# Splitting the attention weights of groups 1 to 3 during attention, in place, in a two-FFN and attention kernel

## The reference

```
x = x + 0.5 * ffn(layernorm(x))        # phase f1
x = x + attention(layernorm(x))        # phase at
x = x + 0.5 * ffn(layernorm(x))        # phase f2

ffn(x): logits = x @ router_w + router_b            # 8 experts, top 2, softmax of the two
        h_e    = silu(x @ expert_w[e] + expert_b[e])
        out    = sum_e(weight_e * h_e) @ proj_w + proj_b
        y = x + out;  return norm_w * y / rms(y)

attention(x): q, k, v = x @ wq.T, x @ wk.T, x @ wv.T    # 16 query heads, 4 kv heads, head dim 128
        q, k = rope(q), rope(k);  k = k * key_weights[head]
        scores = q @ k.T / sqrt(128), causal;  out = (softmax(scores) @ v) @ wo.T
```

## Time and profile before

| | |
|---|---|
| median of 3 runs | 890.74 us |
| the profiled execution | 892.65 us |
| its span, first to last instruction | 890.8 us |
| mean granted TensorE clock | 0.971 |
| busy: PE / DVE / POOL / ACT | 822.6 / 701.0 / 585.2 / 521.4 us |
| phases: f1, attention, f2 | 0 to 171, 171 to 744, 744 to 891 us |
| HBM read and written | 22.02 and 12.58 MB |

### The profile page before, as it was taken

The page is one execution under the profiler, slowest core; times in us unless marked ns, Lnnn a source line. Parts: engine busy times, 40 slices in busy tenths (PEclk is TensorE's granted clock), DMA queues, the critical chain, the costliest instruction groups (busy, mean ns, idle before and its releaser), DMA issues. The chain is left out here.

```text
span 890.8 us, 17017 instructions
## 1 busy us (share of the span) xinstructions
PE 822.6 (92%) x4848; PEld 724.0 (81%) x4848; DVE 701.0 (79%) x1824; ACT 521.4 (59%) x1252; POOL 585.2 (66%) x444
## 2 busy tenths in 40 slices
PE   5998888767999999999999999999999998999984
PEld 4776776656889999999999899899999986787873
DVE  6899989899776776776866867767767797789987
ACT  3654534445765765755865766756767663554542
POOL 3667746368587687777777787777777812556743
PEclk9999988978999999999999999999999999899998
DMA  8053153410212311312312312212212100000001
GB/s 302 1 178 105 72 201 142 142 36 12 49 24 59 106 24 35 94 35 59 94 24 47 94 24 71 85 33 47 71 41 54 25 1 29 1 1 24 24 1 47
DMA packets 26673, 55.98 MB, mean 63 GB/s; under 512 B 3568, under 2 KB 9840, under 8 KB 25104
## 3 DMA queue, kind: packets, MB, share of 16 engines
q1 hardware_dynamic: 26640, 55.59, 21.4%
HBM read 22.02 MB, written 12.58 MB: 39 GB/s over the span
## 5 line engine op out<-in xcount | busy, mean ns | idle before, releaser
L1050 POOL TENSOR_TENSOR at_ql<-at_rot,at_qh 128x512 fp32r<-128x512 f32 x62 | 79.8, 1287 | 99.6 <-ACT at_qh L1272 99.6
L1289 ACT ACTIVATE at_pr<-at_sm,at_low 128x512 f32<-128x512 f32 (+3 forms) x256 | 140.4, 555 | 0.9 <-DVE at_low L1137 0.8
L1295 ACT ACTIVATE at_pth<-at_pt 128x512 fp32r<-128x512 f32 (+1 forms) x192 | 95.8, 525 | 76.0 <-PE at_pt L1449 75.2
L603 ACT ACTIVATE f_s<-f_ex,f_cols 128x512 f32<-128x512 f32 x128 | 84.1, 686 | 86.0 <-PE f_ex L751 46.3
L293 POOL TENSOR_TENSOR f_acc<-f_acc,f_u 128x512 f32<-128x512 f32 x68 | 100.8, 1509 | 40.8 <-DVE f_u L482 27.7
L1147 DVE TENSOR_SCALAR at_pr<-at_pr,at_inv 128x128 f32<-128x128 f32 (+3 forms) x256 | 113.1, 504 | 2.3
L1137 DVE CUSTOM_DVE_ANT_0 at_sm<-at_sc,at_mask 128x512 f32<-128x512 f32 (+3 forms) x256 | 109.8, 484 | 2.5 <-issue 2.4
L1152 DVE TENSOR_TENSOR at_ptl<-at_pt,at_pth 128x512 fp32r<-128x512 f32 (+1 forms) x192 | 108.7, 593 | 1.7 <-ACT at_pth L1295 1.5
L1059 POOL TENSOR_TENSOR at_rot<-ga,cos 128x512 f32<-128x512 f32 x78 | 104.2, 1336 | 4.1 <-POOL at_ql L1050 2.4
L1065 POOL TENSOR_TENSOR at_rot<-at_rot,gc 128x512 f32<-128x512 f32 x78 | 101.5, 1301 | 8.1 <-POOLq L1082 2.1
L1449 PE MATMUL at_pt<-ident,at_pr 128*128 128x128 f32 x640 | 96.3, 278 | 9.3 <-DVE at_pr L1147 6.8
(11 more groups left out here) (212 smaller groups left out, 2262.7 us busy)
## 6 DMA issues: line engine op xcount, KB each, us to landing
gc<-ga SPq DMA_DIRECT2D x160, 128.0 KB, 2.3
ga<-in_attn_w SPq DMA_DIRECT2D x4, 1280.0 KB, 7.7
attn_split<-gb SPq DMA_DIRECT2D x4, 1280.0 KB, 9.6
attn_split<-gc SPq DMA_DIRECT2D x4, 1280.0 KB, 12.1
gb<-attn_split SPq DMA_DIRECT2D x8, 512.0 KB, 4.2
at_wo<-attn_split SPq DMA_DIRECT2D x8, 512.0 KB, 4.3
x<-in_x SPq DMA_DIRECT2D x4, 512.0 KB, 9.0
e_raw<-in_expert_w SPq DMA_DIRECT2D x8, 256.0 KB, 6.7
```

What stands on the lines that cost most here:

```text
L1289: act.activation(pr[h % 2][:, cols], sm[h % 2][:, cols], ACT.Exp, bias=low[h % 2][:, i:i + 1], scale=-1.0, accum_out=tot[h % 2][:, i:i + 1 ...
```

## The change

Group 0 is still split in block 0 of f1, but only its 1536 key, query and value columns, in parts of 512 and 1024, straight into `wa` and `gb`; nothing goes to DRAM. All else is split in attention, in chunks of 512 columns (`CHUNK`) that go through one buffer, `stage`. A group has five: WO_A, WO_B (the two halves of its own wo), and WA, WB_A, WB_B of the next group's key, query and value weights. For each chunk SP loads `stage` after a swap (`load_chunk`, having waited that the chunk before is done), POOL scales the query columns (three of five), ACT copies to hi, DVE subtracts to lo and raises `w_lo`. The host stores the weights in chunks for that. Since chunks sit at fixed steps of a group, the attention loop now runs over groups: 4 steps of group 0, a loop over groups 1 and 2 with 4 steps in it, 4 steps of group 3.

The core of the diff:

```
+        CHUNK_AT = {(0, 1): WO_A, (0, 3): WO_B, (2, 0): WA, (2, 2): WB_A, (3, 0): WB_B}     # (j, h)
...
             def swaps(g, j):                                                                # SP
...
-                    if r == 1 and new_proj is not None:
-                        load_proj(new_proj, wa, FIRST, wa_in)
-                    if r == 3 and new_wo is not None:
-                        load_wo(new_wo)
-                    if r == NR - 1 and new_proj is not None:
-                        load_proj(new_proj, wb, LATER, wb_in)
+                    if j == 0 and r == 0:
+                        load_chunk(g - 1, WB_B)
+                    if j == 0 and r == 3:
+                        load_chunk(g, WO_A)
+                    if j == 1 and r == 4:
+                        load_chunk(g, WO_B)
+                    if j == 2 and r == 2 and more:
+                        load_chunk(g, WA)
+                    if j == 3 and r == 3 and more:
+                        load_chunk(g, WB_A)
...
                 rotate(s, 0)                                                                # POOL, rope(g, j)
+                if j == 0:
+                    scale_chunk(g - 1, WB_B)
                 for r in range(1, NR):
                     rest(s, r - 1)
                     rotate(s, r)
+                    if r == 2 and j == 2 and more:
+                        scale_chunk(g, WA)
+                    if r == 3 and j == 3 and more:
+                        scale_chunk(g, WB_A)
...
+            def chunk_rest(g, k):                                                           # DVE
+                hi, lo = chunk_parts(k)
+                dve.wait_ge(w_hi, chunk_number(g, k) + 1)
+                dve.tensor_tensor(lo, stage[:], hi.bitcast(F32), ALU.subtract).then_inc(w_lo, 1)
...
                     if h == G - 1 and not last:
                         value_rest(s + 1)
+                    if (j, h) in CHUNK_AT and (more or j == 0):
+                        chunk_rest(g, CHUNK_AT[j, h])
...
                     out_lead(n, s, h)                                                       # ACT
                     if more1:
                         prob_lead(n + 1, h1, 2)
+                    if (j, h) in CHUNK_AT and (more or j == 0):
+                        chunk_lead(g, CHUNK_AT[j, h])
                     if h > 0 and ahead:
                         rotated_lead(s + 1, h + 1)
                     if h == G - 1 and ahead:
                         value_lead(s + 1)
...
+            def chunk_split(g, k):                                                          # PE
+                pe.wait_ge(w_lo, chunk_number(g, k) + 1)
...
                 for h in range(G):
+                    if more and j == 2 and h == G - 1:
+                        chunk_split(g, WA)
+                    if more and j == 3 and h == 0:
+                        chunk_split(g, WB_A)
+                    if more and j == 3 and h == 1:
+                        chunk_split(g, WB_B)
+                    if j == 1 and h == 0:
+                        chunk_split(g, WO_B)
                     if more2:
                         scores(n + 2, s if h + 2 < G else s + 1, h2)
...
 # key, query h == 1, output: the waits on wa_in, wb_in and wo_in go
-                pe.wait_ge(wa_in, 32 * (t // BATCH) + WA0)
-                    pe.wait_ge(wb_in, 32 * (t // BATCH) + 32)
-                pe.wait_ge(wo_in, 32 * (s // BATCH) + 32)
...
-                if first:                                                                   # f1: POOL, ACT, DVE
-                    scale_queries(i)
+                if first and not prev:
+                    scale_queries()
-                    if first and e in group_at:
-                        group_lead(i, group_at.index(e))
+                    if first and not prev and e in group_at:
+                        group_lead(group_at.index(e))
-                    if first and e in group_at:
-                        group_rest(i, group_at.index(e))
+                    if first and not prev and e in group_at:
+                        group_rest(group_at.index(e))
```

More of the change, by code:

```diff
@@ L36 @@
 GW = C * QKV + G * D
+CHUNK = SEQ
+CHUNKS = GW // CHUNK
 COLS = C * E + C * D + E * C
@@ L620, in squares, with group_lead @@
                     act.activation(sq[:, t, :], y[:, t, :], ACT.Square, accum_out=ss[:, t:t + 1]).then_inc(sq_done, 1)
[L622 to L628, removed]
+            def group_lead(part):
+                act.wait_ge(a_scaled, (1, 3)[part])
+                act.activation(a_hi[part], a_raw[part], ACT.Copy).then_inc(a_hi_done, 1)
             def step_out(k):
@@ L1001, in _, with load_chunk, swaps @@
         def _(sp):
[L1002 to L1012, removed]
-            def swaps(s, new_wo=None, new_proj=None):
+            def load_chunk(g, k):
+                n = chunk_number(g, k)
+                if not (isinstance(n, int) and n == 0):
+                    sp.wait_ge(w_lo, n)
+                row = (g, CHUNKS - 2 + k) if k in (WO_A, WO_B) else (g + 1, k - WA)
+                sp.dma_start(stage[:], d["attn_w"][bass.ds(row[0], 1), row[1]].rearrange("o p n -> (o p) n")).then_inc(w_raw, 16)
+            def swaps(g, j):
+                s = BATCH * g + j
+                more = not isinstance(g, int) or g < KV - 1
                 for r in range(NR):
@@ L1089, in _ @@
             rstd(1)
-            with pool.Fori(1, STEPS) as s:
-                rest(s - 1, NR - 1)
-                rope(s)
+            for j in range(1, BATCH):
+                rope(0, j)
+            with pool.Fori(1, KV - 1) as g:
+                for j in range(BATCH):
+                    rope(g, j)
+            for j in range(BATCH):
+                rope(KV - 1, j)
             rest(STEPS - 1, NR - 1)
@@ L1299, in out_lead, with chunk_lead, step @@
                 act.activation(out_parts(s, h)[0], o_ps[:], ACT.Copy).then_inc(oh_done, 1)
-            def step(s, first, ahead):
+            def chunk_lead(g, k):
+                n = chunk_number(g, k)
+                act.wait_ge(w_raw, 16 * (n + 1))
+                if k in (WO_A, WO_B):
+                    if not (isinstance(g, int) and g == 0):
+                        act.wait_ge(xu_done, 2 * BATCH * g)
+                else:
+                    act.wait_ge(w_scaled, 3 * g + k - WA + 1)
+                act.activation(chunk_parts(k)[0], stage[:], ACT.Copy).then_inc(w_hi, 1)
+            def step(g, j, first, ahead):
+                s = BATCH * g + j
+                more = not isinstance(g, int) or g < KV - 1
                 for h in range(G):
@@ L1496, in output, with step @@
                     r.then_inc(pj_ready, 1)
-            def step(s, first, ahead):
+            def chunk_split(g, k):
+                pe.wait_ge(w_lo, chunk_number(g, k) + 1)
+            def step(g, j, first, ahead):
+                s = BATCH * g + j
+                more = not isinstance(g, int) or g < KV - 1
                 for h in range(G):
```

203 lines of the change are left out of this document (105 added, 98 removed).

## The result

The changed kernel takes 926.87 us (median, 925.77 to 930.70), beside 890.68 us (890.57 to 891.22) for the kernel before on the same chip: a ratio of 1.0413, 95% interval 1.0382 to 1.0444. It is 36.2 us slower; 28.5 was forecast, and 926.87 lies in the range and at the upper end of the forecast's own. The profiled execution took 927.54 us around a span of 925.7, 34.9 more than the span before.

The account below looks back on a forecast made before the run. The prediction took DVE to fill the first phase and PE alone to bound attention. -10.6 + 2.0 + 14.4 + 8.7 + 14.0 = +28.5 us on 890.7 gave 919.2 us, own range 911 to 927, 8 in 10 903 to 933.

Parts of the forecast that it names:

- WO_B: Step j=1, head 0: PE waits ahead of its scores for DVE's subtraction, 3.6 us in each of four groups, 14.4 us.
- WB_B: Step j=3, head 1: PE waits ahead of its scores for DVE's subtraction, 2.9 us in each of three groups, 8.7 us.
- the other work: Attention: seventeen chunks' copies, subtractions and products fit into ACT, DVE and POOL; with the longer code 2.0 us, 0 to 9.
- the clock: After seven new PE waits in attention the clock falls to 1.2 GHz, 2.0 us each: 14.0 us, 0 to 24.
- The shorter first phase: First feed-forward phase: DVE sheds weight splits, a gain of 10.6 us, between 9.6 and 12.8.
- the last block: Last batch block of the first feed-forward phase: loses between 2.96 and 4.96 us, taken as 3.8.
- Rival 1: Attention: the seven waits come but the clock stays high; 905.2 us, chance 0.15.
- rival 2: Attention: the clock stays low for the long stretch after each wait, 9.8 us more; 929.0 us, chance 0.08.
- The longer code: Attention as more step bodies in a row, with a four-step loop: 0.4 us; by the skill's rule 0 to 2 more.
- Rival 4: Attention's longer code is no longer held, some fifteen more instruction packets hold PE, 14 us more; 933 us, chance 0.05.
- Rival 3: Attention: splits are done before PE reaches the waits, so only the first phase's gain shows; 882.1 us, chance 0.06.
- signs of error: Attention: PE's waits under 1.5 us, the clock staying at 1.00, or other steps growing by more than 0.5 us each.

Follow-up runs that it names:

- e7_narrow: Kernel before, ACT copy and DVE subtraction of groups 1 to 3 in the first phase cut to 16 of 1280 columns, transfers kept: 882.24 us, ratio 0.9894.
- e4_fill: Changed kernel, PE making the coming head's scores once for nothing ahead of the WO_B and WB_B waits: 917.77 us, ratio 1.0300.
- e2_wo: Changed kernel with only the WO_B wait moved to right before the output projection: 913.21 us, ratio 1.0247.
- e5_flat: e1_use with the loop over groups 1 and 2 written out on all engines: 893.58 us, ratio 1.0029.
- e8_afterflat: Changed kernel, early waits kept, with the loop over groups 1 and 2 written out: 925.84 us, ratio 1.0386.
- e9_placedloop: e6_placed with the loop over groups kept, so one jump back per engine: 885.39 us, ratio 0.9925.
- e6_placed: e5_flat with ACT's copies behind rotated query and value, most DVE subtractions ahead of a normalisation, WB_B started a step earlier: 882.24 us, ratio 0.9890.
- e10_actback: e6_placed with ACT's chunk copies put back ahead of the rotated query and the value: 887.45 us, ratio 0.9944.
- e3_wb: Changed kernel with only the WB_B wait moved to right before the query projection of head 1: 915.98 us, ratio 1.0282.
- e1_use: Changed kernel with all four kinds of chunk wait moved to right before the matmuls that read the weights: 896.99 us, ratio 1.0078.

## Why the prediction was right, step by step

The direction, the mechanism and the place were right: seven waits of PE for DVE's subtraction, and a low clock behind them. The sum of 28.5 stands against 34.9 in the spans. That the time still lies inside the forecast's own range, by 0.1 us, is in part luck: the jump and the other work were put some 9 us too low and WB_B 3 too low, while the clock was put 2.5 too high and step 0 happened to be short. Term by term:

- **The shorter first phase**, forecast -10.6, measured -10.66; blocks 1 and 2 took 32.10 and 33.51 us. That the work of splitting fills it, and not the transfers, is shown by e7_narrow. For the last block I wrote 3.8, "the middle" of 2.96 and 4.96; the middle is 3.96.
- **WO_B**, forecast 14.4: 13.8 us of idle, 3.4 to 3.5 each. A step with this wait and no low clock (the last group's) is 37.83, 3.5 over 34.30. Right.
- **WB_B**, forecast 8.7: a step with it and no low clock is 38.2 (e4_fill), 3.9 over; 11.6 for three. Nearly all of the 1.0 us each is the subtraction itself: 1.66 us in the row below, where I had priced it at 0.69 by L1162. DVE and POOL at that place:

```profile
310.92 0.41 DVE L1164 TENSOR_TENSOR at_ptl<-at_pt,at_pth 128x256 fp32r<-128x256 f32 x1
311.25 1.66 DVE L1189 TENSOR_TENSOR gb<-stage,gb 128x512 fp32r<-128x512 f32 x1
```

```profile
311.10 1.26 POOL L1051 TENSOR_TENSOR at_rot<-ga,cos 128x512 f32<-128x512 f32 x1
312.32 1.73 POOL L1053 TENSOR_TENSOR gc<-gc,sin 128x512 f32<-128x512 f32 x1
```

  It begins inside POOL's product, seems to get going when that ends at 312.36, and lasts 0.55 more; POOL's next takes 1.73, where the one after it takes 1.28. The subtraction of L1162 takes one operand from PSUM, this one both from SBUF. The 17 chunk subtractions took 20.7 us, not 11.7. The Trainium skill (SBUF — State Buffer, SBUF: two separate sides) says that a DVE operation with two SBUF inputs and a GpSimd one that reads SBUF share a port pair under an exclusive lock, and whichever starts second fully blocks. These rows agree with it roughly (0.55 us are left of a subtraction of 0.69); no run took POOL's product away. It did not enter my sum, and it should have.
- **The clock**, forecast 14.0 for seven stalls: 11.5 by e4_fill. Six of seven fell, for 1.5 to 2.6 us each. Rival 1 is refuted, and rival 2 as well, since it asked for 3.4 each. The price is not fixed: against the step lengths of e4_fill it was 2.5 to 3.0 us each in e2_wo, where the low clock lasted longer.
- **The longer code**, forecast 0.4: this is the step that was mis-sized. Step 8 is 6.3 us over, of which the excess of an ordinary j = 0 step is 0.6; the other 5.7 are the jump, 2.6 idle and most of the rest a half clock behind it (2.7 by e4_fill). Rival 4 put the price on code that is merely new; that fell, since written-out code (e5_flat, e8_afterflat) has no such stall and on q8 not even more packets, 37. The prediction has the loop before jump thirteen times; over steps 1 to 13 it jumps back twelve times, and no wait of PE is put down to it. The Trainium skill (Runtime: NRT & Kernel Launch, Instruction fetch mechanics) says that prefetch is sequential and that a taken branch to code outside the current window forces a fetch. The place of the stall agrees; that it is a fetch is inferred from the packets. The 0 to 2 us that I had put on it were too little: the step was 4.0 us longer where no clock fell (e9_placedloop), 4.5 and 5.7 where it did.
- **The other work**, forecast 2.0 with the code: the steps without a wait are 34.88 (j = 0) and 35.42 (j = 2), so 5.0 us for steps 0.6 and 1.1 over, the jump apart. "So the work fits", read off ACT's and DVE's idle time, failed: their mean load was never the point. What counts is the place: e6_placed and e10_actback show it, same work, other place, 8.5 us less. Of the j = 0 and 2 steps that make up this term, 0.4 and 0.8 us each went with it. No single long wait of PE stands behind the 1.1 us of a j = 2 step, so which operation is late there was not found.
- **Not in the sum:** step 0 was 2.9 us shorter than before in this profile, where I had counted 0.6 more for the first chunk; the changeover into attention was 0.5 shorter, and what comes behind step 14 0.9 longer.

Together: 14.1 + 11.6 + 11.5 + 5.7 + 5.0 = 47.9 of the 48.1 us in steps 1 to 14; with the first phase and the last point, +34.9. Rival 3 is refuted by the waits. Of what I named as signs of error one came true: the other steps grew by more than 0.5 each, 0.6 with j = 0 and 1.1 with j = 2, and step 8 most of all.

## What to carry to other kernels

Put a wait right before the matmul that reads the data; queued half a head too early it cost here 3.4 to 3.9 us of idle and, where the clock fell, 1.4 to 3.0 more, on an engine without slack. When work moves onto engines that have idle time, look at what stands behind it in their queues and at what runs beside it on POOL at that moment, not at their busy share. Price a loop by its jump back when its body is long; here a loop of two turns, with one jump, saved no time and made one step 4 to 6 us longer.

## What the runs showed of the hardware

- Idles of PE of 3.4 to 3.9 us in otherwise dense matmuls were followed by 1.2 GHz in six of seven cases in the changed kernel, and in all fourteen of e2_wo (3), e3_wb (4) and e8_afterflat (7); idles of 1.5 to 1.8 us at the same places never were (e4_fill, seven cases). Of the idles at the jump four were (2.58 us in the changed kernel, 2.56 in e1_use, 2.75 in e2_wo, 2.71 in e3_wb); one of 2.71 (e4_fill) and two of 2.06 and 1.40 close together (e9_placedloop) were not. So the same idle at the same place may or may not bring the clock down. Behind the wait in step 13, where the changed kernel kept its clock, e8_afterflat lost it, and the step took 39.48 us and not 37.83:

```profile
680.40:683.80 3.40, 3.40 (x17) 3.30 (x16) 2.12 (x9) 0.86 (x2) 2.20 (x2) 0.51 0.00 0
```

- Step 0 is not steady: 47.45 and 48.30 us in two profiles, 51.24 to 54.15 in the others. DVE is busiest in it (46.38 us of 47.45 in e10_actback, 49.54 of 51.84 in e6_placed). DVE's normalisation in these two, mean duration in ns last but one:

```profile
L1160 DVE TENSOR_SCALAR at_pr<-at_pr,at_inv 128x128 f32<-128x128 f32 (+3 forms) x24 | 13.7, 633 | 0.2
```

```profile
L1160 DVE TENSOR_SCALAR at_pr<-at_pr,at_inv 128x128 f32<-128x128 f32 (+3 forms) x24 | 16.1, 733 | 0.2
```

  The same 24 operations take 100 ns more each in one case, 2.4 of the 4.4 us between the two steps. The cause was not tested, and whether it makes the several us between runs of one kernel is not shown.
